# A hand-scheduled attention and expert block on one core: the layout products of z move to the bank of the weighted values, and the two tables of steps are laid out anew

## The chip, the cores and the metric

One NeuronCore of a Trainium2 chip runs the whole program. TensorE (PE) multiplies, VectorE (DVE), ScalarE (ACT) and GpSimd (POOL) do the rest, SyncE (SP) starts most transfers. The metric is the device time of one execution in microseconds, the median of several runs; less is better.

## The reference

Two stages follow each other on x of 2 x 1024 tokens with 256 features, and all of it is float32:

```python
# first stage: cross-attention to 154 context rows, 16 heads of 16
xq  = ada_ln(x, cond);  xkv = ada_ln(ctx, cond)
q = xq @ Wq + bq;  k, v = split(xkv @ Wkv + bkv)
x = x + (softmax(q k^T / 4) v) @ Wp + bp
# second stage: evidence from the same context, a router and three experts
nx = layer_norm(x) * gamma + beta
w  = softmax((nx @ Wq2) (ctx @ Wk2)^T / 16);  evidence = w (ctx @ Wv2)
c  = concat(nx, evidence, cond)
p  = softmax(c @ router_W + router_b)
y  = sum_e p_e * (silu(c @ e_w1[e] + e_b1) @ e_w2[e] + e_b2)
g  = sigmoid(silu(c @ gate_w1 + gate_b1) @ gate_w2 + gate_b2)
x  = x + g * (y @ out_w + out_b)
```

## The kernel before, in words

The 2048 tokens are cut into 4 chunks of 512 tokens, a chunk into 4 blocks of 128. The first stage handles the 16 heads of a chunk in 4 groups of 4, so there are 16 groups `g`. Everything is planned by hand. `PARTS` gives each kind of step a letter and lists its steps in order; a string of letters is a table of steps. Every engine walks the same table with `walk` and does its own share of each step, so that the table alone sets the order of the work on all engines. Between engines there are semaphores only, and each engine works strictly in order.

The letters that matter here, with what PE does and who answers:

- `P` projects the queries of a group (six 128x512 products in two steps), ACT and DVE make the query halves (L734, L1042). `R` (`rows`) computes row scores of one block into the two banks `pair` (L1377), and DVE takes their maximum (L1032); the next `R` waits for it. `S` (`shift`) adds the four maxima to the queries' bank (L1385), DVE makes the shifted queries. `K` (`keys`) computes scores by key into one of two banks, ACT exponentiates (L744); a `K` waits for the exponential of the `K` two before. `A` (`av`) sums the values weighted by the exponentials into the bank `B_U` (`bank4`; L1417, L1420), and ACT copies it to `u` (L753).
- `u` (`uz`) transposes one block's `u` (L1432), DVE divides and writes `z` (L1050, L1053). `z` (`ztr`) transposes that `z` (L1443), ACT copies it to `zt` (L759). `w` (`wproj`) multiplies `zt` by Wp, DVE adds it to x (L1059). These three are the layout products and the output product of a block, 16 blocks in all.
- `f` (`prep`, 29 of them) prepares weights of the second stage, `x` transposes a normalised chunk, `m` and `t` make the tables of the evidence product, `L`, `l`, `N` the second layer norm, `C`, `E`, `W`, `T`, `p` the evidence weights, `o` the router. `H` (`hidden`) is one of 14 blocks of a chunk's first expert layer (ten 128x512 products), `h` (`hsplit`) splits its result in two on DVE and POOL, `D` (`part`) is its second layer (twelve 128x256 products), `U`, `B`, `Z` sum and finish. `X`, `a`, `e` (`scale`, `gated`, `last`) finish the last chunk.

PSUM has eight banks. `B_TOK` (`bank5`) is shared by `f`, `x`, the first four `m`, and by `u`, `z` and `w` of the first 12 blocks. On PE the function `take_tok` guards it: whoever takes the bank first waits until the last user's result has been read. The last four blocks alternate between `B_TOK` and `B_U` (`tok_bank`). `B_U` belongs to `A` alone until then.

There are three tables: `L0_ORDER` (first stage and what was woven in), `BETWEEN_ORDER` (the passage: the last four blocks of the first stage, the evidence tables, the first evidence weights), `L1_ORDER` (the second stage). After `BETWEEN_ORDER` the first `H` needs, among other things, the low parts of the evidence tables that POOL moves between partitions with two DMAs (`m_ev<-m_ev`, L614). PE's products all go through the helper `passes`, so most of them have the line L1269.

Of the kernel before, what the change touches and what calls it, by code (L numbers as in the profile page):

```python
# [83 lines left out]
def build(nc, dram, out):  # L84
    ctx = ExitStack()
    with ctx:
# [244 lines left out]
        def y_tile(j):  # L331
# [4 lines left out]
            "s": [("split", c, h) for c in range(0, NC) for h in range(2)],  # L336
            "c": [("kc", gi) for gi in range(NG)],
            "V": [("val", n) for n in range(2)],
            "r": [("kr", gi) for gi in range(NG)],
            "P": [("proj", g, k) for g in range(GR) for k in range(KC)],  # L340
            "f": [("prep", n) for n in range(len(PREP))],
            "R": [("rows", g, q) for g in range(GR) for q in range(TJ)],
            "q": [("wq", 1)],
            "S": [("shift", g) for g in range(GR)],
            "K": [("keys", g, k) for g in range(GR) for k in range(GH + 1)],
            "b": [("stats", c, h) for c in range(1, NC) for h in range(2)],
            "g": [("rsqrt", c) for c in range(1, NC)],
            "A": [("av", g) for g in range(GR)],
            "n": [("norm", c, h) for c in range(1, NC) for h in range(2)],
            "y": [("second", n) for n in range(6)],  # L350
            "x": [("xt", c, h) for c in range(1, NC) for h in range(2)],
            "u": [("uz", n) for n in range(TJ * NC)],
            "z": [("zt", n) for n in range(TJ * NC)],
            "w": [("wp", n) for n in range(TJ * NC)],
            "m": [("m", n) for n in range(len(MP))],
            "t": [("m_taken", n) for n in range(len(MP))],
            "L": [("ln_stats", c) for c in range(NC)],
# [6 lines left out]
            "T": [("wtr", n) for n in range(TJ * NC)],  # L364
            "p": [("wsplit", c) for c in range(NC)],
            "o": [("router", c) for c in range(NC)],
            "H": [("hidden", c, m) for c in range(NC) for m in HORD],
            "i": [("w2_split", e) for e in range(E)],
            "h": [("hsplit", c, m) for c in range(NC) for m in range(HB)],
            "G": [("gate", n) for n in range(TJ * NC)],  # L370
            "D": [("part", c, m) for c in range(NC) for m in range(HB)],
            "B": [("bias", c, e) for c in range(NC - 1) for e in range(E)] + [("bias", NC - 1, e) for e in (0, 2, 1)],
# [6 lines left out]
        L0_ORDER = (  # L379
            "sscVcrPPfRqfRcVRcrPfPRfSffrrKRbKfRKKfRPKRbfPSfgRKA"  # L380
            "fKRPKKKRfRnA"
            "SfPyfKxnKRyKRxysKRKfRA"
            "sSPPfKPRKKfRyKyfKbRA"
            "yRfPSuKKRKuPKRzPfRwRbKSzA"
            "uKRKwPguKRKzKRPnwRA"
            "zSwnRKxKRKsxKRKsfA"
            "RPSPfKfRPKRKfKRbKfRPA"
            "SfKKRuKRKuKRzPRwPuSA"
            "zbRPzgRKwRKKwKRuKnPSzKnRxA"
            "wKRKxsKRsKfRPPSmtKA"  # L390
            "KRKfKRKmRA"
            "RPtPSfRKKuKRKzKRwPLPRuA"
            "SRzKKwKRKuPKRzlPwRuSRA"
            "KzRKKRKwRKA"
            "SmltNKKFtNmKCKCKEWEA"
            "CC"
        )
        BETWEEN_ORDER = (
            "TuWmztmuw"
            "mEWtmEtTzTWmtw"  # L400
            "Tputtmmztw"
            "umzotw"
        )
        L1_ORDER = (
            "H"
            "LlH"
            "H"
            "H"
            "NihGlhiDGihhH"
            "H"  # L410
            "NFBH"
            "GH"
            "hEDCGDCUhUUUEDH"
            "EWBCDH"
            "hCDWTH"
            "ThDWH"
            "hUUEUDhUH"
            "DWTDhpThLBH"
            "lUZH"
            "H"  # L420
            "DhUUH"
            "DH"
            "GNloUFhZH"
            "hNGDH"
            "H"
            "hZZDGhBDH"
            "ChUCUDUWEEUH"
            "hWH"
            "GH"
            "hCDTEBCWDhUH"  # L430
            "DhUUUWTDTEH"
            "poDTDhhLBUUH"
            "H"
            "DH"
            "lZDGhZH"
            "lH"
            "UGNUhH"
            "FNZH"
            "hDCZH"
            "CEhBhDH"  # L440
            "WDDGUhH"
            "UUUBEH"
            "EDEGhCCWDH"
            "hWUTUhUUDDH"
            "WhpTH"
            "TBTDH"
            "hoH"
            "DhH"
            "DUUDUH"
            "ZhZUGH"  # L450
            "hH"
            "ZhH"
            "GDZDhDBGUUH"
            "DH"
            "hUH"
            "UDH"
            "BH"
            "hDhBDhUXhDH"
            "H"
            "UUhhGUXH"  # L460
            "aXXhaaeaDeDeeDD"
        )
        part_of = {letter: iter(steps) for letter, steps in PARTS.items()}
        L0_STEPS = [next(part_of[letter]) for letter in L0_ORDER]
        BETWEEN_STEPS = [next(part_of[letter]) for letter in BETWEEN_ORDER]
# [57 lines left out]
        def _(pool):  # L523
# [85 lines left out]
            walk(L0_STEPS, {"xt": xb, "keys": keys, "av": av, "rsqrt": newton, "ln_stats": lambda c: newton(NC + c)})  # L609


            pool.wait_ge(m_h, m_hi(MTAIL))
# [646 lines left out]
        def _(pe):  # L1259
# [412 lines left out]
```

## Time and profile before

| | |
|---|---|
| time, 3 runs | 469.65, 471.16, 471.36 us; median 471.16 |
| time of the profiled execution | 471.39 us |
| its span (first to last instruction) | 469.6 us |
| PE busy | 445.7 us, 95% |
| DVE, ACT, POOL busy | 314.5, 215.5, 149.4 us |
| from the first key projection to the first `H` | 21.27 to 239.85 us |
| second stage on PE | 239.85 to 464.1 us |

The profiled execution took 1.8 us more than its span. A PE that is shown busy is one that has a product in flight: the busy time of a product reaches past the moment at which the next one may start.

### The profile page before, as it was taken

To read this page: it belongs to the slowest core of one execution; us is meant where nothing else is said; L and a number is where in the kernel's file an instruction comes from. 1 tells how busy PE (TensorE), PEld (TensorE's weight loads), DVE (VectorE), ACT (ScalarE), POOL (GpSimd) and SP (SyncE) were. 2 spreads that over 40 slices of the span, in tenths; PEclk is the share of its full clock that TensorE was granted. 3 is DMA by queue.
4 is the path that set the end of the run, shared out by engine and by line. 5 is a ranking of instruction groups with operands and counts; after the bars stand their busy time and mean duration, and the time that the engine had idled before them with its cause. 6 is when DMAs were issued, how large, how long until landed. Compare 5 with 4: busy or idle time off the path is not lost.

```text
span 469.6 us, 7042 instructions
## 1 busy us (share of the span) xinstructions
PE 445.7 (95%) x2396; PEld 345.7 (74%) x2396; DVE 314.5 (67%) x822; ACT 215.5 (46%) x377; POOL 149.4 (32%) x233
## 2 busy tenths in 40 slices
PE   7989889998999999999989999999999999999995
PEld 6866546665766657655468988889898889888885
DVE  5487676778568748858967687567776496733634
ACT  2466766455445545455432464254482355522220
POOL 4000263347343301200033224345225432334436
PEclk8599999999999999999999999999999999999998
DMA  8910411200220000000020000001000010001001
GB/s 285 398 29 1 156 46 46 68 24 22 68 67 3 0 1 0 1 1 1 0 75 1 1 0 1 1 1 46 0 1 1 1 45 1 1 1 45 1 0 46
DMA packets 7314, 17.50 MB, mean 37 GB/s; under 512 B 752, under 2 KB 2288, under 8 KB 7152
## 3 DMA queue, kind: packets, MB, share of 16 engines
q1 hardware_dynamic: 6336, 13.84, 8.4%
q0 software_dynamic: 656, 2.29, 1.7%
q10 hardware_dynamic: 288, 0.92, 0.5%
q8 instruction: 20, 0.33, 0.3%
q14 instruction: 14, 0.11, 0.1%
HBM read 14.50 MB, written 2.10 MB: 35 GB/s over the span
## 4 chain that ended last, share of the span: by engine, by line
PE 85%; DVE 5%; ACT 3%; DMA 2%; issue 2%; POOL 1%; POOLq 0%; SPq 0%; DVEq 0%; ACTq 0%
PE bank L1269 55%; PE pair L1269 14%; PE pair L1377 4%; PE bank L1420 3%; PE bank L1417 3%; DVE xq L1042 2%; DVE nm L1032 2%; DMA wss_sb<-in_wss 1%; PE bank L1432 1%; PE bank L1284 1%; PE bank L1385 1%; ACT xq L734 1%; DMA m_ev<-m_ev 1%; PE bank L1443 1%; ACT kc L680 1%
## 5 line engine op out<-in xcount | busy, mean ns | idle before, releaser
L620 POOL TENSOR_TENSOR hs<-hid,hs 128x512 fp32r<-128x512 f32 x48 | 63.4, 1320 | 114.7 <-DVE hs L1202 114.7
L1269 PE MATMUL bank<-nx,w1h 128*128 128x512 f32 x224 | 72.6, 405 | 0.2 <-DMA m_ev<-m_ev 0.2
L1269 PE MATMUL pair<-w2h,hs 128*128 128x256 f32 x384 | 72.1, 287 | 0.0
L1032 DVE TENSOR_REDUCE nm<-pair 128x4 fp32r<-128x616 f32 x64 | 51.1, 798 | 20.1 <-PE pair L1377 19.3
L1269 PEld LDWEIGHTS pair<-w2h,hs 128*128 128x128 f32 x384 | 60.9, 189 | 2.1 <-POOL hs L620 0.2
L815 ACT ACTIVATE hid<-bank,ab 128x512 f32<-128x512 f32 x48 | 33.0, 688 | 62.0 <-PE bank L1269 61.5
L1269 PE MATMUL pair<-w2l,hs 128*128 128x256 f32 x192 | 54.1, 282 | 0.0
L744 ACT ACTIVATE pt<-bank 128x512 f32<-128x512 f32 x72 | 41.0, 597 | 21.7 <-PE bank L1269 21.2
L1269 PEld LDWEIGHTS bank<-nx,w1h 128*128 128x128 f32 x224 | 39.9, 189 | 7.7 <-issue 0.8
L1269 PE MATMUL bank<-nx,w1l 128*128 128x512 f32 x112 | 44.2, 394 | 0.0
L1269 PE MATMUL bank<-wh,m_ev 128*128 128x512 f32 x112 | 44.1, 394 | 0.0
L1269 PE MATMUL bank<-xq,keys 128*128 128x512 f32 x96 | 39.6, 452 | 2.0 <-DVE xq L1042 1.6
L1377 PE MATMUL pair<-keys,xq 128*128 128x308 f32 x128 | 33.9, 346 | 5.4 <-DVE nm L1032 3.8
L1202 DVE CAST hs<-hid 128x512 fp32r<-128x512 f32 x48 | 22.7, 473 | 20.5 <-ACT hid L815 14.8
L1269 PEld LDWEIGHTS pair<-w2l,hs 128*128 128x128 f32 x192 | 36.1, 188 | 0.0
L1222 DVE SCALAR_TENSOR_TENSOR acc<-pair,pr,acc 128x256 f32<-128x256 f32 x44 | 19.6, 479 | 21.5 <-PE pair L1269 21.5
L1377 PEld LDWEIGHTS pair<-keys,xq 128*128 128x128 f32 x128 | 21.5, 189 | 16.5 <-issue 12.4
L568 POOL MEMSET xq<- 64x512 f32 x14 | 7.3, 520 | 81.0 <-PE bank L1269 80.9
L734 ACT ACTIVATE xq<-bank,small_sb 64x512 fp32r<-64x512 f32 x32 | 21.9, 683 | 20.1 <-PE bank L1269 19.6
L1042 DVE SCALAR_TENSOR_TENSOR xq<-bank,small_sb,xq 64x512 fp32r<-64x512 f32 x32 | 24.0, 750 | 9.1 <-PE bank L1385 8.3
L1269 PEld LDWEIGHTS bank<-wh,m_ev 128*128 128x128 f32 x112 | 21.0, 188 | 5.0
L1269 PEld LDWEIGHTS bank<-nx,w1l 128*128 128x128 f32 x112 | 21.0, 188 | 4.9
(209 smaller groups left out, 897.0 us busy)
## 6 DMA issues: line engine op xcount, KB each, us to landing
stage<-in_w1n POOLq DMA_DIRECT2D x7, 256.0 KB, 3.3
w1e_sb<-in_w1e SPq DMA_DIRECT2D x1, 1792.0 KB, 6.8
x_sb<-in_x SPq DMA_DIRECT2D x3, 512.0 KB, 10.3
stage<-in_w1a SPq DMA_DIRECT2D x3, 512.0 KB, 11.3
stage<-in_ew2T SPq DMA_DIRECT2D x3, 512.0 KB, 3.8
out_x<-x_sb SPq DMA_DIRECT2D x3, 512.0 KB, 2.6
wss_sb<-in_wss SPq DMA_DIRECT2D x2, 512.0 KB, 7.3
x_sb<-in_x ACTq DMA_DIRECT2D x1, 512.0 KB, 5.0
```

The lines of the kernel that those rows point to most:

```text
L620: g_.tensor_tensor(hs[:, q % 3, 1, :], hid[:, q % 2, :], hs[:, q % 3, 0, :], ALU.subtract).then_inc(hl_r, 1)
L734: A(xq[r, g % 2, s_, :], B_P[g % 2][r, :], ACT.Identity, bias=small[r, SM["bq"][0] + g % NG:SM["bq"][0] + g % NG + 1]).then_inc(qh_r, 1)
L744: A(weight(g, k), B_ST[n % 2][:, :], ACT.Exp, scale=DH ** -0.5).then_inc(ex_d, 1)
L815: A(dst, B_H[n % 2][:, :], ACT.Silu, bias=ab1[:, m, c // CPB:c // CPB + 1]).then_inc(h_r, 1)
L1032: V.tensor_reduce(nm[:, g % 2, q, :].rearrange("p (h w) -> p h w", w=32)[:, :, DH:DH + 1], pair[:, :, 0:2 * LK].rearrange("p s (a n) -> p ...
L1042: V.scalar_tensor_tensor(xq[low, g % 2, s_, :], B_P[g % 2][r, :], small[r, SM["bq"][0] + g % NG:SM["bq"][0] + g % NG + 1], xq[r, g % 2, s_ ...
L1202: V.tensor_copy(hs[:, q % 3, 0, :], hid[:, q % 2, :]).then_inc(hh_r, 1)
L1222: V.scalar_tensor_tensor(acc[:, j, :], y_tile(j), pr[:, c % 2, j, e:e + 1], acc[:, j, :], ALU.mult, ALU.add).then_inc(y_r, 1)
L1269: ins = mm(dst, a, b_, start=first and i == 0, stop=last and i == len(terms) - 1, skip_group_check=free)
L1377: ins = mm(B_S[s][:, 0:2 * LK], xq[:, g % 2, s, P * q:P * q + P], kr[c // CPB][:, gi, 2 * LK * s:2 * LK * (s + 1)], start=True, stop=True)
L1417: mm(B_U[32 * j:32 * j + 32, :], vmain[:, b, GH * gi + j, :], weight(g, j), start=True, stop=False, skip_group_check=True)
L1420: mm(B_U[:, :], vtail[:, b, gi, :], weight(g, GH), start=False, stop=True, skip_group_check=True).then_inc(av_d, 1)
```

## The change

The transposes of z (`ztr`) of the first 12 blocks write to `B_U` instead of `B_TOK`. On PE, `B_U` gets a guard of its own, `take_u`, used by `av` and by these transposes: each waits until ACT has read what the last user left there. The first two tables become one, `EARLY_ORDER`, and both tables have a new order; the order of the letters in `PARTS` has no effect. `gated` names one more wait on DVE, for the gate's tanh. The steps themselves are the same: each engine executes the same instructions on the same shapes.

```diff
         def tok_bank(n, step):
-            return B_TOK if n < LAST else (B_TOK, B_U)[(3 * (n - LAST) + step) % 2]
+            return (B_U if step == 1 else B_TOK) if n < LAST else (B_TOK, B_U)[(3 * (n - LAST) + step) % 2]
...
-        L0_ORDER = (
-            "sscVcrPPfRqfRcVRcrPfPRfSffrrKRbKfRKKfRPKRbfPSfgRKA"
...
-        BETWEEN_ORDER = (
...
+        EARLY_ORDER = (
+            "ssVcVrqPPfRbcfRcfRbcPfRrPSfRrgfKRKfKKRfrKRfPPSfKRKA"
...
+            "CtETCmuWmtzmtEuwtmTzmWouwttmztmwutTTptmzw"
         )
         L1_ORDER = (
...
             def gated(j):
 
                 dve.wait_ge(y_r, TJ * (E * NC - 2) + j + 1)
+                dve.wait_ge(th_r, TJ * (NC - 1) + j + 1)
...
+            ub = [None, None]
+
+            def take_u(freed, value):
+
+                if ub[0] is not None:
+                    pe.wait_ge(ub[0], ub[1])
+                ub[0], ub[1] = freed, value
...
                 if g == 0:
                     pe.wait_ge(v_r, B)
                     pe.wait_ge(ones_r, 1)
-                else:
-                    pe.wait_ge(u_r, g)
+                take_u(u_r, g + 1)
...
             def ztr(n):
                 if n < LAST:
-                    take_tok(zt_r, n + 1)
+                    take_u(zt_r, n + 1)
                 else:
                     pe.wait_ge(x1_r, n)
```

On every engine one walk replaces the walks of `L0_STEPS` and `BETWEEN_STEPS`.

**PE, first chunk.** The rows below are those of PE where the first blocks are turned while groups 4 and 5 run; `negI,nm` is a shift, `xq,keys0` a key score, `pair<-keys0,xq` a row score, `pt,vmain` and `pt,vtail` an `A`, `ident_sb,u` a `u`, `ident_sb,z` a `z`, `wp_sb,zt` a `w`. Before:

```order
L1269 MATMUL bank2<-xq,keys0 128x512 x2
L1385 MATMUL bank1<-negI,nm 128x128 x4
L1443 MATMUL bank5<-ident_sb,z 128x128 x2
L1417 MATMUL bank4<-pt,vmain 32x512 x4
L1420 MATMUL bank4<-pt,vtail 128x512
L1432 MATMUL bank5<-ident_sb,u 128x128 x4
L1269 MATMUL bank3<-xq,keys0 128x512
L1377 MATMUL pair<-keys0,xq 128x308 x2
L1269 MATMUL bank2<-xq,keys0 128x512
L1269 MATMUL bank5<-wp_sb,zt 128x256 x2
L1269 MATMUL bank1<-xh,wqh 128x512
```

The same place of the changed kernel:

```order
L1431 MATMUL bank5<-ident_sb,u 128x128 x4
L1385 MATMUL bank1<-negI,nm 128x128 x4
L1442 MATMUL bank4<-ident_sb,z 128x128 x2
L1377 MATMUL pair<-keys0,xq 128x308 x2
L1431 MATMUL bank5<-ident_sb,u 128x128 x4
L1416 MATMUL bank4<-pt,vmain 32x512 x4
L1419 MATMUL bank4<-pt,vtail 128x512
L1261 MATMUL bank3<-xq,keys0 128x512
L1377 MATMUL pair<-keys0,xq 128x308 x2
L1261 MATMUL bank5<-wp_sb,zt 128x256 x2
L1442 MATMUL bank4<-ident_sb,z 128x128 x2
```

The transposes of z stand in `bank4`, in turns with `A`, and a `u` may now follow a `u` in `bank5` with the `z` of the first between them.

**PE, the end of the passage.** The rows in front of the first `H` (`nx0,w1h`); `w1e_sb,vt` 64x256 is the last tail piece, whose result goes through ACT and POOL's two DMAs to the first `H`, and `ident_sb,pn` with `pn3` is a `T`. Before:

```order
L1269 MATMUL bank2<-w1e_sb,vt 64x256 x2
L1443 MATMUL bank4<-ident_sb,z 128x128 x2
L1269 MATMUL bank5<-wp_sb,zt 128x256 x2
L1432 MATMUL bank4<-ident_sb,u 128x128 x4
L1269 MATMUL bank3<-w1e_sb,vf 128x256 x2
L1443 MATMUL bank5<-ident_sb,z 128x128 x2
L1269 MATMUL bank4<-wp_sb,zt 128x256 x2
L1269 MATMUL bank2<-nx0,w1h 128x512 x2
```

The same place of the changed kernel:

```order
L1261 MATMUL bank2<-w1e_sb,vt 64x256 x2
L1261 MATMUL bank5<-wp_sb,zt 128x256 x2
L1431 MATMUL bank4<-ident_sb,u 128x128 x4
L1549 MATMUL pair<-ident_sb,pn 128x128
L1550 MATMUL pair<-ident_sb,pn3 96x128
L1549 MATMUL pair<-ident_sb,pn 128x128
L1550 MATMUL pair<-ident_sb,pn3 96x128
L1261 MATMUL bank3<-w1e_sb,vf 128x256 x2
L1442 MATMUL bank5<-ident_sb,z 128x128 x2
L1261 MATMUL bank4<-wp_sb,zt 128x256 x2
L1261 MATMUL bank2<-nx0,w1h 128x512 x2
```

Two `T` have moved in behind the tail piece, and the transpose of z that stood right behind it has moved ahead of it.

**DVE, the end of the program.** `acc<-th,acc` is a `gated`, `acc<-pair,lsc` a `last`, the cast the last `hsplit`; POOL adds to x in the same order. Before:

```order
L1235 TENSOR_SCALAR lsc<-th,pr 128x256 x2
L1202 CAST hs<-hid 128x512
L1240 SCALAR_TENSOR_TENSOR acc<-th,acc 128x256 x2
L1247 TENSOR_TENSOR acc<-pair,lsc 128x256
L1240 SCALAR_TENSOR_TENSOR acc<-th,acc 128x256
L1247 TENSOR_TENSOR acc<-pair,lsc 128x256 x3
```

The same place of the changed kernel:

```order
L1227 TENSOR_SCALAR lsc<-th,pr 128x256
L1233 SCALAR_TENSOR_TENSOR acc<-th,acc 128x256
L1194 CAST hs<-hid 128x512
L1233 SCALAR_TENSOR_TENSOR acc<-th,acc 128x256
L1240 TENSOR_TENSOR acc<-pair,lsc 128x256 x4
```

The last `gated` stands ahead of all four `last`, and the third one ahead of the last cast.

## Rows read from the trace of the kernel before

**Rows 1.** Page, busy time of each engine over the span, with instructions

```profile
PE 445.7 (95%) x2396; PEld 345.7 (74%) x2396; DVE 314.5 (67%) x822; ACT 215.5 (46%) x377; POOL 149.4 (32%) x233
```

**Rows 2.** Windows: start:end, width, then PE, PEld, DVE, ACT, POOL busy, clock

```profile
233.70:239.85 6.15, 4.38 (x22) 2.91 (x21) 5.23 (x17) 2.77 (x7) 1.13 (x2) 1.00 0.32 76
239.85:464.10 224.25, 224.21 (x1296) 196.81 (x1296) 141.33 (x404) 89.16 (x136) 83.52 (x100) 1.00 0.03 10
...
21.27:239.85 218.58, 203.05 (x1034) 133.47 (x1033) 161.57 (x361) 120.45 (x232) 56.90 (x115) 1.00 0.11 35
```

**Rows 3.** Waits of PE between 21 and 240 us: total, times, longest

```profile
PE pair L1377 <- DVE nm L1032: 3.8, 8, 0.8
PE bank L1269 <- DVE xq L1042: 1.6, 3, 0.9
...
PE bank L1420 <- ACT pt L744: 0.2, 1, 0.2
```

**Rows 4.** Timeline of group 4: start, duration, engine and line, waits in brackets

```profile
88.25 1.53 DVE L1042 SCALAR_TENSOR_TENSOR xq<-bank,small_sb,xq 64x512 fp32r<-64x512 f32 x2 [0.88 <-PE bank L1385]
89.05 0.73 PE L1269 MATMUL bank<-xq,keys 128*128 128x512 f32 x2 [0.38 <-DVE xq L1042]
89.59 1.09 ACT L744 ACTIVATE pt<-bank 128x512 f32<-128x512 f32 x2 [0.35 <-PE bank L1269]
...
92.08 0.45 PE L1377 MATMUL pair<-keys,xq 128*128 128x308 f32 x2
...
92.36 0.38 PE L1443 MATMUL bank<-ident_sb,z 128*128 128x128 f32 x2
...
92.56 0.80 DVE L1032 TENSOR_REDUCE nm<-pair 128x4 fp32r<-128x616 f32 x1 [0.50 <-PE pair L1377]
```

**Rows 5.** Groups by shape: count, busy time and mean ns, idle before

```profile
L744 ACT ACTIVATE pt<-bank 128x512 f32<-128x512 f32 x72 | 41.0, 597 | 21.7 <-PE bank L1269 21.2
...
L753 ACT ACTIVATE u<-bank 128x512 f32<-128x512 f32 x16 | 9.6, 598 | 26.4 <-PE bank L1420 26.4
...
L759 ACT ACTIVATE zt<-bank 128x256 f32<-128x256 f32 x16 | 6.1, 383 | 9.2 <-PE bank L1443 9.2
```

**Rows 6.** Timeline of the end of the passage

```profile
233.67 0.44 PE L1443 MATMUL bank<-ident_sb,z 128*128 128x128 f32 x2
...
234.43 0.36 ACT L769 ACTIVATE m_ev<-bank 32x256 fp32r<-32x256 f32 x1
...
234.81 0.38 ACT L770 ACTIVATE m_ev<-bank 32x256 fp32r<-32x256 f32 x1
...
235.55 0.60 PE L1432 MATMUL bank<-ident_sb,u 128*128 128x128 f32 x4
...
235.99 1.03 PE L1269 MATMUL bank<-w1e_sb,vf 128*128 128x256 f32 x4
...
239.85 0.70 PE L1269 MATMUL bank<-nx,w1h 128*128 128x512 f32 x2 [0.20 <-DMA m_ev<-m_ev]
```

**Rows 7.** Chain that ended last, pieces of it: start, us, what

```profile
236.40 3.31 DMA m_ev<-m_ev
...
286.19 2.32 PE bank L1269 x10
288.50 1.43 PE pair L1269 x12
```

**Rows 8.** Chain that ended last, behind the last product

```profile
463.89 0.83 POOL x_sb L637
464.73 0.68 POOL x_sb L631
465.41 0.68 POOL x_sb L637
```

**Rows 9.** The four `gated` on DVE: min/median/max ns, first and last start

```profile
L1240 DVE SCALAR_TENSOR_TENSOR acc<-th,acc x4: 415/416/1517, 457.8 to 463.7; 128x256 f32<-128x256 f32 x4
```

**Rows 10.** Timeline of POOL, the last `hsplit`

```profile
460.39 1.41 POOL L620 TENSOR_TENSOR hs<-hid,hs 128x512 fp32r<-128x512 f32 x1 [1.31 <-DVE hs L1202]
```

More of the change, by code:

```diff
@@ L364, in build @@
             "T": [("wtr", n) for n in range(TJ * NC)],
+            "o": [("router", c) for c in range(NC)],
             "p": [("wsplit", c) for c in range(NC)],
-            "o": [("router", c) for c in range(NC)],
             "H": [("hidden", c, m) for c in range(NC) for m in HORD],
@@ L428, in build @@
[L428 to L450, printed above, removed]
@@ L451, in build @@
-            "hH"
[L452 to L461, printed above, removed]
+            "LH"
+            "iH"
+            "H"
+            "hllH"
+            "hBFH"
+            "hNDNH"
+            "CiECGDhWWUH"
+            "H"
+            "EhDDUhGEUCCUBH"
+            "iEhH"
+            "GDTDhTWWH"
+            "UUhLDhUDUH"
+            "TH"
@@ new lines, in build @@
+            "pTlH"
+            "DBlH"
+            "hhGoNH"
+            "FhNH"
+            "DDUH"
+            "EUhEUDCUZCH"
+            "H"
+            "DH"
+            "DZWH"
+            "TWhH"
+            "hZZhBGEhEUDhUDCUCUTH"
+            "WBGhWH"
+            "DDH"
+            "hLhGphUUUDH"
+            "UlTTDH"
+            "GlDhBNUDH"
+            "oFUDDZNH"
+            "ZH"
+            "hCEUCH"
+            "hUGH"
+            "H"
+            "H"
+            "DhDZWEZhDCBH"
@@ L462, in build @@
+            "UhUCUDETUWH"
+            "hhH"
+            "GTH"
+            "EGDDhBH"
+            "WUWDhDUUpTH"
+            "TH"
+            "hUGoDH"
+            "hDH"
+            "H"
+            "DhDhBUUUH"
+            "ZGUhhZH"
+            "H"
+            "DZGDhhH"
+            "GZH"
+            "XDBUUUDGhH"
+            "UH"
+            "DH"
+            "BDBXH"
+            "DDH"
+            "hH"
+            "hhDhDXUDUaahUUXahDaeeee"
         )
         part_of = {letter: iter(steps) for letter, steps in PARTS.items()}
-        L0_STEPS = [next(part_of[letter]) for letter in L0_ORDER]
@@ L465, in build @@
-        BETWEEN_STEPS = [next(part_of[letter]) for letter in BETWEEN_ORDER]
+        EARLY_STEPS = [next(part_of[letter]) for letter in EARLY_ORDER]
         L1_STEPS = [next(part_of[letter]) for letter in L1_ORDER]
@@ L1251, in _ @@
             out_parts = {"uz": uz, "wp": wproj, "m_taken": mpiece}
[L1252 removed]
+            walk(EARLY_STEPS, {"kc": kc_, "kr": place, "wq": wq_split, "second": second, "val": val, "stats": chunk_stats, "rsqrt": chunk_rsqrt, "norm": norm, "split": xsplit, "rows": rows, "shift": shift, "prep": prep,
                               **out_parts, **front_parts})
[L1254 removed]
             walk(L1_STEPS, {"gate": gate, "w2_split": w2_split, "hsplit": hsplit, "bias": bias, "sum": expert_sum, "final": final, "scale": scale, "gated": gated, "last": last, **front_parts})
```

79 lines of the change are left out of this document (26 added, 53 removed).

## The prediction

> **What bounds the kernel now.** The page comes first: PE is busy 445.7 of 469.6 us, 95%, and DVE 67% [rows 1]. One number for the whole program hides two stages, so the windows come next. From the first `H` to PE's last product it is busy 224.21 of 224.25 us [rows 2]: the second stage is PE's own work, and an order can't shorten it unless it opens gaps. The early part, from the first key projection to the first `H`, lasts 218.58 us, of which PE is busy 203.05 [rows 2]. Its 15.5 us of visible gaps are what a new order can win.
>
> More is lost there than shows. The chain has ten 128x512 products in 2.32 us and twelve 128x256 products in 1.43 us [rows 7], so their slots are 0.23 and 0.12 us. The timeline shows a 128x512 product alone as 0.40 us and more: the last 0.17 us of it lie under the next one's slot when there is no gap. A gap of PE is therefore about 0.17 us longer than it is drawn.
>
> Then the waits: no single one rules. The largest kind is the row score behind DVE's maximum, 3.8 us in 8 waits; the shifted queries have 1.6 us in 3, the copy of `zt` 1.4 us in 3 [rows 3]. Fourteen kinds with some 28 waits make up PE's idle time. So this is a kernel of many small replies that come a little late, and I judge the new table by how much work PE has between a question and its answer.
>
> **The early table: cover.** I take slots as above (0.14 us for a row-score product, from 92.08 to 92.36 for two [rows 4]; others read in the same way) and a reply time for each kind of handover, from the end of the asking slot. Row scores ask until 92.36, and the maximum runs from 92.56 for 0.80 us [rows 4]; with the start of the next product and some queue on DVE I take 1.3 us. A key score asks at 89.28, ACT's exponential starts at 89.59 and takes 0.60 [rows 4, 5]: 1.15 us. A shift is answered by DVE's 0.77 us, and PE goes on 1.0 us later when it waits (88.05 to 89.05 [rows 4]): 1.3 us with some queue. Of the token bank I take 0.9 us behind a `z` (0.38 on ACT [rows 5]) or a `w`, 1.2 behind a `u`, 1.0 behind a preparation, 1.6 behind a transpose of x. Then I go through both orders and add PE's slots between question and answer:
>
> - row score to the next row score, 63 handovers: 23 are short of 1.3 us before and 15 after, the sum of what is missing 10.1 us before and 4.1 after;
> - key score to the second next, 78: 19 short before, 6 after, 6.4 and 1.9 us;
> - shift to the first key score, 16: 7 and 3, 3.8 and 2.4 us;
> - last row score to shift, 16: 5 and 10, 2.2 and 4.0 us, the one kind that gets worse;
> - projection to the first row score: 7 and 9, 6.1 and 5.1 us;
> - from one user of the token bank to the next: 76 takings before, of which 42 short by 16.8 us together; 64 after (the 12 transposes of z are gone), 24 short by 5.4 us;
> - `B_U`: 15 before, none short; 27 after, 3 short by 0.5 us.
>
> A step that waits for several things counts once, with the largest lack: 48.6 us before, 25.5 after, 48% less. The sum is no time, since a gap that one wait opens covers the next. The scale comes from the trace: without the last 6.15 us, PE's gaps in the early part are (218.58 - 6.15) - (203.05 - 4.38) = 13.8 us, and with 0.17 us each for about 27 waits 18.4 us. If gaps fell in proportion, 8.7 us would go. They won't quite: a gap that vanishes takes cover from its neighbours, and DVE, busy 161.6 of 218.6 us here [rows 2], has its replies pushed closer together. Averaged over stretches of 10 us of PE work, what DVE or ACT has to do beyond PE is even slightly more in the new table than in the old. I take a little over half: **4.8 us**. Bounds: 0 (gaps only move) and 8.7 us.
>
> **The end of the passage.** Before, the last tail piece of the evidence table is multiplied until 233.67, its copies on ACT wait for a transpose's copy and end at 235.19, POOL starts the DMAs, the chain has their 3.31 us from 236.40, and the first `H` starts at 239.85, with 0.20 us of waiting for them [rows 6, 7]: 4.66 us from ACT's end, 6.18 from the product's. PE's work in these 6.18 us is only about 3.5 us (two `w`, two `z`, a `u`, the last product), the rest are waits for `z` and `zt`. In the new order the transpose is ahead of the tail piece, so ACT can begin 0.2 us after it instead of 0.76: 0.2 + 0.36 + 0.38 + 4.66 = 5.6 us. The two `T` moved in give 3.7 us of work, so the transfer becomes what ends last here, and PE should wait for it visibly, up to about 1 us. Gain: 0.5 us in the path and 0.2 us of work that is now under it, **0.7 us** (from 0 to 1.0). The evidence weights, split on ACT and DVE only behind the second `T`, take some 3.2 us with the `zt` copy behind them, from 2 us after the tail product: they are in time by 0.4 us, and would be next in line.
>
> **The second stage.** The same instructions, and at least as much cover for most (the closest `hidden` to its `part` has 4.2 us of work between them in place of 3.6). Before, nothing shows but 0.04 us. 0, and up to 1 us lost.
>
> **The tail.** Behind the last product the chain is POOL's: a `last` of 0.83 us, the fourth `gated` of 0.68, another `last` [rows 8]. The new order has that `gated` ahead of all `last`, and its DVE part too: **0.7 us** off the path. Against it stands that the third `gated` is now ahead of the last cast on DVE. A `gated` takes 0.416 us, but one took 1.517 [rows 9], started at 460.2, while POOL subtracted from 460.39 for 1.41 us [rows 10]. If that hits the third, the cast, POOL's subtraction and the last `part` are late by 1.1 us, less about 0.5 us of room. The term is then 0.7 - 0.6 = 0.1 us. I take 0.7, since by the order POOL has nothing to do when it starts. The Trainium skill has a rule on this that speaks against the change: by "GPSIMD Engine Reference", section "Specifications", GpSimd's SBUF interface is shared with VectorE and contends with DVE instructions that have two SBUF inputs, which a `gated` is. The trace agrees with its 1.517 against 0.416 us; the rule alone would make the tail 0.1 us, the order of the two engines 0.7.
>
> **Sum.** 4.8 + 0.7 + 0 + 0.7 = 6.2 us off 471.4, the profiled execution's own time (span 469.6 and 1.8 around it), 465.2. The median of the runs shown is 0.2 lower, 471.16. I predict 465.4 us.
>
> **Rivals.**
>
> *The gaps only move.* The new order has no less to do for DVE and ACT, and the replies have queues behind them which my counts don't know; the kind that gets worse, row score to shift, is in each of the 16 groups. For it: DVE's load, 74% of the early part [rows 2]. Against it: nearly every kind has more cover at once. Then only 0 to 0.7 us of the early table, and the rest: 471.2 - 1.5 = 469.7 us. Measured as no change (a difference under 0.5%, 2.4 us, is about what can't be told).
>
> *`B_U` becomes the queue.* Now `A` waits for a copy of `zt` and `z` for the copy of `u` (0.598 us [rows 5]), on an ACT that has exponentials of 0.597 us in its queue. Six of the 27 handovers have under 1.4 us of cover (0.7 to 1.38, 1.0 in the mean). With two exponentials ahead of the copy the answer takes 0.17 + 3 x 0.6 = 2.0 us, 1 us late, 6 us in all, and each delays an `A` with its whole group. It decides from the point at which such queues are the rule and the early table gains less than 3.6 us: with no gain in it 471.2 + 6 - 1.4 = 475.8, with a small one 474 us. Against it: before, ACT waits 26.4 us for PE's `A` [rows 5], so it is mostly free at that moment.
>
> *All of the cover counts.* The gaps fall in proportion or beyond, as they would if the short row scores also delayed everything behind them: 8.7 to 10 us, with 1.4 us for the ends: 461 us. Against it: DVE would then be at 77% in the early part.
>
> *The change does nothing by its bank.* The bank alone lifts the wait of a `z` for the token bank only where a `z` was short (10 of its takings, 3.2 us of lack); if the gain is there, most of it comes from the order. This shifts no time here.
>
> **How the numbers follow.** My forecast, 462.5 to 468.5, has 0.56; gaps that move, 469 to 471.5, 0.20; the queue on `B_U`, 472 to 476, 0.10; all of the cover, 459.5 to 462.5, 0.14. The first and the last are faster by over 0.5% (under 468.8): 0.70. Same 0.20, slower 0.10. The range leaves out the slow rival and the far end of the fast one: 460.5 to 471.3.
>
> **What would show it.** Right: the first `H` starts at about 234.4 us (239.85 - 5.5), PE's idle time in the early part falls from 15.5 to about 11 us; its waits for DVE's maximum are fewer; a wait of PE for `m_ev` of 0.3 to 1 us stands in front of the first `H`; 224.2 us follow with PE full; from PE's end to the end 4.8 us in place of 5.5, with no L1233 between the POOL pieces of the chain. Wrong: waits of `A` or `z` for ACT's `u` and `zt` of more than 2 us together (the queue), or the same idle time with other names (moved gaps), or gaps in the second stage.

## The result, and the profile after

The changed kernel takes 457.18 us (median of 4 runs, 456.38 to 458.20) against 471.16: a ratio of 0.9725, 95% interval [0.9674, 0.9775]. The forecast was 465.4, in a range of 460.5 to 471.3. The direction was right, the gain of 14 us was over twice the forecast 6.2, and the time lies below the range.

The windows of the profiled execution (458.2 us, span 456.2), columns as in [rows 2]; the first three rows go from PE's first product of the early table and from the first row score to the first `H`, and from there to PE's last product:

```profile
21.27:227.54 206.27, 198.67 (x1033) 136.12 (x1033) 163.18 (x362) 120.25 (x231) 56.31 (x115) 0.99 0.12 37
29.48:227.54 198.06, 190.96 (x1004) 130.08 (x1003) 156.88 (x346) 115.37 (x221) 56.31 (x115) 0.99 0.11 34
227.54:451.50 223.96, 223.95 (x1296) 196.88 (x1296) 145.53 (x403) 88.26 (x135) 85.09 (x101) 1.00 0.03 10
...
57.00:61.10 4.10, 2.43 (x12) 1.68 (x12) 3.33 (x6) 2.83 (x6) 3.31 (x6) 1.00 0.01 4
61.20:64.60 3.40, 3.40 (x13) 2.65 (x11) 1.83 (x3) 2.27 (x4) 0.50 (x1) 0.50 0.00 0
```

The early part lost 12.3 us (218.58 to 206.27), all behind the prologue. Two things stand out. PE's gaps fell from 15.5 to 7.6 us, which is only 7.9 of the 12.3: its busy time fell as well, from 203.05 to 198.67 us, for the same products. And from 61.2 to 64.6 us the granted clock is 0.50, the lower of its two levels, so 1.7 us are lost in a stretch that the kernel before doesn't have.

The waits of PE in the whole program:

```profile
PE pair L1377 <- DVE nm L1024: 2.5, 4, 1.5
...
PE bank L1261 <- DVE kc L959: 0.9, 2, 0.8
PE bank L1385 <- DVE nm L1024: 0.7, 2, 0.5
PE bank L1261 <- DMA m_ev<-m_ev: 0.7, 1, 0.7
PE bank L1261 <- ACT zt L752: 0.6, 1, 0.6
```

The maximum still leads, in 4 waits in place of 8 [rows 3]. No wait for ACT's `u` or for `B_U` is on the list. The chain that ended last, at the end of the passage and behind the last product:

```profile
222.49 0.38 ACT m_ev L763
...
223.48 0.60 POOL m_ev L607
...
224.09 3.32 DMA m_ev<-m_ev
...
227.54 1.63 PE bank L1261 x6
```

```profile
450.82 0.44 DVE acc L1240
...
451.32 1.40 POOL x_sb L630 x2
452.73 0.68 POOLq L86
453.41 0.68 POOL x_sb L630
```

ACT's second copy starts at 222.49 and the DMA ends 4.9 us later; the tail has no `gated` between its `last` pieces and takes 4.7 us in place of 5.5.

### The profile page after: what moved, and what is told of

It is laid out like the page before. It is cut to its first block, busy times and chain, and to the rows that moved or that the text cites. A ratio compares the mean times of both kernels' runs of the same rounds, so it can differ in the third digit from the quotient of the medians.

```text
span 456.2 us, 7055 instructions
## 1 busy us (share of the span) xinstructions
PE 441.0 (97%) x2396; PEld 348.5 (76%) x2396; DVE 320.0 (70%) x822; ACT 214.4 (47%) x377; POOL 149.6 (33%) x233
## 4 chain that ended last, share of the span: by engine, by line
PE 89%; DVE 4%; DMA 2%; ACT 2%; issue 1%; POOL 1%; POOLq 0%; SPq 0%; DVEq 0%
PE bank L1261 55%; PE pair L1261 15%; PE pair L1377 4%; PE bank L1419 3%; PE bank L1416 3%; DMA wss_sb<-in_wss 2%; PE bank L1431 2%; PE bank L1385 1%; ACT kc L673 1%; DVE nm L1024 1%; PE bank L1276 1%; PE bank L1316 1%; DVE kc L959 1%; DMA m_ev<-m_ev 1%; PE bank L1442 1%
## 5 line engine op out<-in xcount | busy, mean ns | idle before, releaser
L1194 DVE CAST hs<-hid 128x512 fp32r<-128x512 f32 x48 | 21.6, 458 | 34.3 <-ACT hid L808 22.3
L1261 PE MATMUL bank<-xq,keys 128*128 128x512 f32 x96 | 39.4, 466 | 0.2
L1377 PE MATMUL pair<-keys,xq 128*128 128x308 f32 x128 | 35.2, 357 | 2.9 <-DVE nm L1024 2.5
L727 ACT ACTIVATE xq<-bank,small_sb 64x512 fp32r<-64x512 f32 x32 | 21.8, 682 | 18.9 <-PE bank L1261 18.4
```

The costliest lines, as they stand in the source:

```text
L727: A(xq[r, g % 2, s_, :], B_P[g % 2][r, :], ACT.Identity, bias=small[r, SM["bq"][0] + g % NG:SM["bq"][0] + g % NG + 1]).then_inc(qh_r, 1)
L1194: V.tensor_copy(hs[:, q % 3, 0, :], hid[:, q % 2, :]).then_inc(hh_r, 1)
L1261: ins = mm(dst, a, b_, start=first and i == 0, stop=last and i == len(terms) - 1, skip_group_check=free)
L1377: ins = mm(B_S[s][:, 0:2 * LK], xq[:, g % 2, s, P * q:P * q + P], kr[c // CPB][:, gi, 2 * LK * s:2 * LK * (s + 1)], start=True, stop=True)
```

## A measure for the loss, used below

The experiments are compared on one stretch, from the first row score to the first `H`: 211.06 us before, 198.06 after. The prologue is left out, since its length differs between runs of one and the same kernel: the clock is at its lower level there for a time that varies. The windows of before, and of an experiment with the new order:

```profile
10.00:15.00 5.00, 5.00 (x19) 3.96 (x19) 4.24 (x22) 0.11 (x1) 0.00 (x0) 0.50 1.04 404
15.00:20.00 5.00, 5.00 (x22) 4.60 (x22) 0.99 (x5) 2.23 (x6) 0.00 (x0) 0.50 1.05 396
```

```profile
10.00:15.00 5.00, 5.00 (x24) 4.03 (x24) 4.14 (x22) 0.98 (x3) 0.00 (x0) 0.66 1.05 405
15.00:20.00 5.00, 5.00 (x25) 4.38 (x25) 2.25 (x8) 3.29 (x8) 0.00 (x0) 0.69 1.05 396
```

The first is the kernel before, the second order_only. In the profiled executions this lower level lasts from 3.4 to 13.7 us, which at half the speed is up to 5.1 us of time; 30 runs of the kernel before on one chip went from 466.42 (mean clock 0.993) to 471.59 us (0.982). Ahead of the first record of the clock, 4.3 to 7.3 us into the full kernels, 128x512 products start 0.43 us apart instead of 0.23, so PE is at the lower level there too; this time isn't in these figures.

What PE would need without any late reply was measured by itself (`pe_alone`, below): 182.24 us for this stretch in the old order, 180.82 in the new. The difference to the full kernel is its **loss**. "Lack" is the sum of missing cover by the forecast's count, "low" the time at the lower clock inside the stretch, of which half is lost; it is 1.7 us wherever 3.4 stands.

| kernel | ratio to before, 95% | stretch, us | low | loss | lack |
|---|---|---|---|---|---|
| before | 1 | 211.06 | 0 | 28.8 | 48.6 |
| changed | 0.9725 [0.9674, 0.9775] | 198.06 | 3.4 | 17.2 | 25.5 |
| changed_again | 0.9694 [0.9624, 0.9764] | 198.33 | 3.4 | 17.5 | 25.5 |
| bank_only | 1.0074 [1.0042, 1.0106] | 215.54 | 3.4 | 33.3 | 51.0 |
| order_only | 0.9917 [0.9881, 0.9953] | 207.10 | 3.4 | 26.3 | 36.2 |
| late_only | 0.9997 [0.9960, 1.0034] | 211.03 | 0 | 28.8 | 48.6 |
| new_to_a8 | 0.9900 [0.9863, 0.9938] | 204.45 | 0 | about 23 | 39.4 |
| norm_later | 0.9700 [0.9648, 0.9752] | 198.22 | 3.4 | 17.4 | 25.5 |
| short_max_before | 0.9931 [0.9897, 0.9964] | 206.72 | 0 | 24.5 | 38.1 |
| short_max_after | 0.9617 [0.9565, 0.9669] | 194.85 | 3.4 | 14.0 | 18.4 |
| climbed | 0.9676 [0.9623, 0.9729] | 196.19 | 0 | about 15 | 25.0 |
| least_lack | 0.9727 [0.9672, 0.9783] | 196.75 | 0 | 16.0 | 15.6 |
| one_bank_least | 0.9954 [0.9917, 0.9990] | 210.66 | 0 | about 29 | 31.0 |

("About": the order was not run alone, and 181 or 182 us are taken for it.)

Since PE's products come in one order, the loss can be taken apart: for each product, the distance to the one before it in the full kernel less the same distance in PE alone, summed by the step that the product belongs to. Worked out from the starts of some 790 products (those that start together counted once) (in us; `R` row scores, `K` key scores, `S` shifts, `prep` preparations; `rest` has projections, table pieces, scores and the first `H`):

```
                    R    K    S    A  prep   u    z    w    x  rest   sum
before             8.5  4.0  0.5  0.2  6.6  1.9  1.6  2.7  0.4  2.4  28.8
bank_only          8.2  3.8  0.5  2.3  6.6  2.8  3.8  2.3  0.7  2.4  33.3
short_max_before   2.1  4.7  0.1  0.6  7.7  2.2  1.6  3.0  0.4  2.0  24.5
order_only         5.9  1.1  1.4  0.1  3.6  2.2  6.2  2.4  1.8  1.6  26.3
changed            6.6  1.1  1.6  0.1  3.3  0.7  0.1  1.7  0.5  1.5  17.2
short_max_after    3.8  1.7  0.4  0.1  3.6  0.7  0.0  1.5  0.5  1.8  14.0
least_lack         4.4  0.8  0.9  0.1  5.1  0.7  1.3  1.1  0.5  1.1  16.0
```

## The experiments

**The bank without the order, the order without the bank.** In both, one half of the change; the bank's half is

```diff
-            return B_TOK if n < LAST else (B_TOK, B_U)[(3 * (n - LAST) + step) % 2]
+            return (B_U if step == 1 else B_TOK) if n < LAST else (B_TOK, B_U)[(3 * (n - LAST) + step) % 2]
```

> The kernel before with one thing of the change: the twelve layout products of z below the last chunk write to `B_U` and take it in turn with `A`; both tables keep the order of before, and the fourth `gated` waits for the hyperbolic tangent as in the changed kernel. Theory *cover*: what counts is how much PE work lies between a question and its answer. In the old order z on `B_U` relieves the token bank but its neighbours on `B_U` are now too close (4.3 us of lack appear there), so the sum of what is missing goes from 48.6 to 51.0 us; at the 0.5 us of time per us of lack that the pair of kernels shows (11.7 us for 48.6 - 25.5 = 23.1 us), 1.2 us slower: 472.4 us, between 471 and 474. Rival *bank*: the token bank's queue was the cause, and the new order only follows it: then most of the 14 us is here already, under 463 us.

> The changed kernel with one thing taken back: the layout products of z use the token bank again, in both tables' new order. Theory *cover*: in this order 64 takings become 76, and z stands close to `u` and `w`, so the lack goes from 25.5 to 36.2 us, and at 0.5 us per us 5.4 us of the gain are lost: 457.2 + 5.4 = 462.6 us, between 460 and 465. PE's waits for the copies of `zt` and of z then show in the trace. Rival *bank*: without the second bank the new order gains next to nothing: over 468 us. Rival *order alone*: the bank's place doesn't matter, 457 to 459 us.

The bank alone made the kernel 0.7% slower: the queue on `B_U` that the prediction named as a rival is real in the old order. Its waits of PE (the experiments' line numbers are 64 below those of the changed kernel, as their tables stand on fewer lines):

```profile
PE bank L1378 <- ACT u L682: 1.8, 3, 0.7
...
PE bank L1352 <- ACT zt L688: 1.4, 1, 1.4
```

The first is a `z` behind the copy of `u`, the second an `A` (here L1352) behind the copy of `zt`, and a slow stretch of the clock follows it at 97.0 us (that the wait brought it is not shown):

```profile
95.00:97.00 2.00, 0.57 (x7) 0.31 (x11) 1.90 (x6) 1.72 (x4) 1.81 (x3) 1.00 0.04 8
97.00:100.40 3.40, 3.40 (x10) 0.73 (x3) 0.28 (x1) 0.00 (x0) 1.30 (x2) 0.50 0.29 75
```

```profile
96.82 1.83 PE L1352 MATMUL bank<-pt,vmain 128*32 128x512 f32 x8 [1.43 <-ACT zt L688]
98.59 2.01 PE L1355 MATMUL bank<-pt,vtail 128*128 128x512 f32 x2
```

The order alone gives 0.8%, less than the 462.6 us expected (1.8%). Without the bank, `z` (L1378) waits for DVE's division (L981), which also frees the token bank of the `u` before it, and for the residual addition, `u` (L1367) and x (L1252) for `zt`:

```profile
PE bank L1378 <- DVE z L981: 2.1, 4, 0.8
PE bank L1378 <- DVE x_sb L987: 1.6, 3, 0.8
...
PE bank L1367 <- ACT zt L688: 1.1, 2, 0.8
PE bank L1252 <- ACT zt L688: 1.1, 1, 1.1
```

So the two halves are no sum: on this stretch +4.5 and -4.0 us alone, -13.0 together (without the slow stretches of the clock +2.8, -5.7 and -14.7). The new table puts `u`, `z` and `w` close to one another, which needs the second bank; the old one puts `z` right ahead of `A`, where the second bank hurts. The rival that the bank alone is the cause and the rival that it doesn't matter both fall.

**The second table alone, and the new order up to the eighth `A`.**

> The kernel before with the second table of the changed kernel only, and its wait in `gated`; early tables and bank of before. Theory: the second stage is PE's own work in either order, and only the tail gets shorter, by the `gated` that POOL no longer does between its `last` pieces: 471.2 - 0.8 = 470.4 us, between 469.7 and 471; in the trace PE's end lies 4.7 us before the end of the span, in place of 5.5. Rival: part of the gain of 13 us lies in the second table, below 468 us.

> A table that follows the new order up to the eighth `A` and then has the steps that are left in the old order, z on `B_U`, second table of before. Theory *cover*: the sum of lack is 39.4 us, 9.2 less than before, so at 0.5 us per us 4.7 us faster: 466.5 us, between 464.5 and 468.5. Rival *one place*: the gain stems from one stretch (the first half, say); then this kernel has all of it (under 460) or none (over 470).

The second table leaves the time where it was within [0.9960, 1.0034], too wide for 0.8 us; its profile has 223.95 us in the second stage and, from PE's last start to the end, 5.1 us in place of 5.8. With the new order up to the eighth `A`, 1.0% is gained, as expected, and 6.6 of the 13.0 us of the stretch: half of the gain lies up to there and half behind it, not all in one place.

**The long wait of the new table.** At 58 to 60 us the largest wait is left. The timeline of the changed kernel:

```profile
54.61 0.74 DVE L876 TENSOR_SCALAR lnt<-x_sb,mv,rs 128x256 f32<-128x256 f32 x2
...
57.80 0.39 DVE L959 SCALAR_TENSOR_TENSOR kc<-bank,small_sb,klo 64x154 fp32r<-64x154 f32 x1
...
58.22 1.41 DVE L876 TENSOR_SCALAR lnt<-x_sb,mv,rs 128x256 f32<-128x256 f32 x2
...
59.65 0.80 DVE L1024 TENSOR_REDUCE nm<-pair 128x4 fp32r<-128x616 f32 x1
...
60.60 0.52 PE L1377 MATMUL pair<-keys,xq 128*128 128x308 f32 x2 [1.49 <-DVE nm L1024]
```

```diff
-            "nKRfnRKKPfRPxSRKKfyKRssxA"
+            "nKRfRnKKPfRPxSRKKfyKRssxA"
```

> The changed kernel itself once more, beside the kernel before on the same chip, since the profiles show PE's clock at its lower level for a stretch of the prologue whose length differs from run to run (3.4 us up to 13.7 us), and once more at 61.2 to 64.6 us in the changed kernel, behind a wait of 1.5 us. Theory: that second stretch belongs to the kernel's order and comes again; 457 us, 2.9% below the kernel before, with 189.4 us from the first shift to the first `H` (201.4 before). Rival: it is chance; without it the same stretch of the program takes 187.7 us.

> The changed kernel with one letter of the early table moved: the normalising of the second half of chunk 1 behind the row score (2,2), no longer ahead of it. In the changed kernel it took 1.41 us on DVE there, and PE waited 1.49 us for the maximum behind it, after which the granted clock was 0.5 for 3.4 us. Theory *wait and clock*: the 1.5 us of waiting go and with them the slow stretch, which costs as much again (3.4 us at half the speed, 1.7 us): together 3 us less than the changed kernel, 454 us. Rival *the wait only*: 1.4 us less. Rival *it moves*: the normalising delays the next reply by as much, no change.

The changed kernel came out the same on another chip, slow stretch included (55.6 us, since the prologue was shorter). Moving the letter did what the third rival said: the wait for the maximum went, and one of the same size came at the transposes of x, whose bank waits for the key block that DVE now makes later. Between 40 and 70 us:

```profile
PE bank L1252 <- DVE kc L895: 1.2, 1, 1.2
PE bank L1197 <- DVE kc L895: 1.0, 2, 0.8
PE pair L1313 <- DVE nm L960: 0.6, 2, 0.4
```

**A shorter maximum, with both orders untouched.**

```diff
-                                pair[:, :, 0:2 * LK].rearrange("p s (a n) -> p s a n", a=2), AXX, ALU.max).then_inc(mx_d, 1)
+                                pair[:, :, 0:2 * LK].rearrange("p s (a n) -> p s a n", a=2)[:, :, :, 0:38], AXX, ALU.max).then_inc(mx_d, 1)
```

> The kernel before with the row maximum taken over 38 of the 154 keys of a head (so it leaves out part of the maximum, which sets only the shift of the exponentials). The maximum takes 0.80 us, this one should take some 0.25, so every answer to a row score comes 0.55 us sooner, with the order untouched. Theory *cover*: what is missing falls from 48.6 to 38.1 us, at 0.57 us of time per us of lack (13.1 us for 23.1, the changed kernel without its slow stretch) 6.0 us faster: 465 us against 471. Rival *DVE is no cause*: PE's gaps come from elsewhere, under 2 us. Rival *DVE's queue*: 35 us less of DVE's work help every other reply too, over 9 us.

> The same shortened row maximum (38 of 154 keys, part of the maximum left out) in the changed kernel. Theory *cover*: the new order already covers most of the row scores, so less is left to win: the lack falls from 25.5 to 18.4 us, 4.0 us faster, and the slow stretch behind the wait of 1.5 us may go as well (1.7 us): 451 to 453 us. Rival: as much as in the kernel before or more, and then the new order's gain has nothing to do with how late the maxima are.

The maximum by groups, before and then shortened with the old order:

```profile
L1032 DVE TENSOR_REDUCE nm<-pair 128x4 fp32r<-128x616 f32 x64 | 51.1, 798 | 20.1 <-PE pair L1377 19.3
...
L1032 DVE TENSOR_REDUCE nm<-pair 128x4 fp32r<-128x152 f32 x64 | 20.1, 314 | 22.3 <-PE pair L1377 21.5
```

0.31 us in place of 0.80, and the stretch is 4.3 us shorter with the old order, 3.2 to 3.5 with the new. Expected were 6.0 and 4.0. With the old order neither rival holds, under 2 us or over 9; with the new one the gain is less than with the old, so its rival falls too. The row scores alone lose 6.4 us less (8.5 to 2.1), and a third of it, net, comes back, 1.1 at the preparations, 0.7 at the key scores, 0.3 to 0.4 each at `u`, `w` and `A`: this is the cover that a vanished gap takes from its neighbours. The table also says that the row scores lose nearly as much in the new order as in the old (6.6 and 8.5), though by the count their lack had fallen by 7 us.

**PE alone.** All blocks but PE's are taken out; DVE clears two shared tiles and raises every semaphore by 100, then PE's program runs as it stands.

```diff
+            for s in SEMS:
+                nc.vector.memset(flag[:], 0.0).then_inc(s, 100)
+                dve.wait_ge(s, 100)
```

> PE's program of the kernel before, with all its waits, and nothing else: no other engine computes, all operands are zeros in two shared tiles, every semaphore is raised far enough before PE starts, so each wait is answered long before it is asked (the kernel computes nothing of the reference; it leaves out all work of the other engines). It gives the time of PE's own slots, which the timeline of the full kernel can't show. Theory *late replies*: from the first shift to the first `H` 160 us, against 201.4 in the full kernel: 41 us are late replies, not the 18.4 of the forecast. Rival *the forecast's scale*: about 183 us, and the loss is what the drawn gaps say.

> The same for the changed kernel: PE's program with all its waits, every one answered before it is asked, all work of the other engines left out. Theory *late replies*: within 2.5 us of the order of before (158 to 160 us from the first shift to the first `H`), so the new order gains by replies and not by PE's own work. Rival *PE's own slots*: what stands next to what on PE sets the cost (a waiting step behind a transpose, say), and the new order is quicker by 5 us or more here already.

> As the one before, but without the waits of PE's program (only the first, for the zeros). The difference is what waits cost that are answered long before: about 320 more instructions for waits in PE's queue. Theory: some 0.08 us for each step with two waits or more, as a row score behind a key score starts 0.31 us after it in place of 0.23, so 10 to 20 us shorter over the whole program, most of it in the early part. Rival: waits that are answered cost nothing, no difference.

The windows of the stretch, in this order of kernels, the first with its second stage below it:

```profile
59.09:241.32 182.23, 182.23 (x1008) 130.25 (x1007) 0.00 (x0) 0.00 (x0) 1.00 0.00 1
241.32:464.80 223.48, 223.48 (x1298) 197.68 (x1296) 0.00 (x0) 0.00 (x0) 1.00 0.00 1
```

```profile
63.14:243.96 180.82, 180.82 (x1004) 129.49 (x1003) 0.00 (x0) 0.00 (x0) 1.00 0.00 1
```

```profile
60.39:241.19 180.80, 180.80 (x1004) 129.48 (x1003) 0.00 (x0) 0.00 (x0) 1.00 0.00 1
```

From the first shift on it is 173.7 and 173.2 us. My 160 was wrong, and so was the forecast's scale. The two orders differ by 1.4 us in PE's own slots, and a wait that is answered costs nothing (180.82 against 180.80), against my theory of 10 to 20 us. The row to look at beside it is that of the full kernel before:

```profile
28.79:239.85 211.06, 196.82 (x1007) 128.44 (x1007) 155.91 (x346) 114.13 (x218) 56.90 (x115) 1.00 0.10 32
```

PE counts as busy for 196.82 us there, where PE alone is busy 182.23 with the same products. So of the 28.8 us lost, 14.2 are drawn as gaps and 14.6 hide under the drawn ends of products.

PE alone also differs in that the other engines are still and its operands are zeros, so a rival is that they slow PE's products themselves. The starts speak against it. In the second stage, where DVE, ACT and POOL work too, the full kernel takes 224.25 us [rows 2] and PE alone 223.48, and of 1296 products 3 start more than 0.02 us late, 0.2 us together; in the changed kernel none does. In the early part 860 of 1006 products of the kernel before start within 0.02 us of their distance in PE alone, and all 49 that are late by more than 0.17 us are products whose weight load waits for a semaphore. Each of the programs with PE alone was executed once, so 1.4 us between two orders rests on one execution of each; the two in the new order and the one of least_lack, below, agree within 0.1 us.

**A table with the tangle at 56 to 60 us undone.** The letters of that place, changed kernel and experiment:

```
"...KRfPPSfKRKA"  "nKRfnRKKPfRPxSRKKfyKRssxA"
"...KRfPPSRnfKKA" "RfnKRKPfRKPxSRKKfsyKRsxA"
```

> The changed kernel with some twenty letters of the early table moved by one to five places, most of them between 38 and 62 us: the score products of group 1 go on while DVE and ACT prepare the keys of the second batch, and their placing stands apart from the row maxima. By the count of cover nothing changes: 25.0 us are missing in place of 25.5, 0.3 us faster. Theory *count*: 0 to 1 us faster than the changed kernel. Rival *queues*: the count knows no queues on DVE and ACT; where several replies stand behind one another on DVE (key blocks, normalising, maximum at 56 to 60 us), untangling them gives 3 to 5 us, and with no gap of over a microsecond the slow stretch of the clock goes as well.

The stretch is 196.19 us with no slow part: 2.1 less than changed_again, of which 1.7 are the clock. In the ratio (0.9676 against 0.9694) it can't be told from the changed kernel. What was left at this place wasn't 3 to 5 us.

**Tables made by the count itself.** By then loss over lack, with the 1.7 us of the slow stretches taken off, was 0.58 to 0.68 in every kernel. The next tables were made by lowering the lack alone; their expectations are the most informative misses of this study.

> The changed kernel with an early table in which 72 of 379 letters stand elsewhere, each by a few places, chosen for nothing but a smaller sum of missing cover, by the reply times of the forecast: 15.6 us are missing in place of 25.5 (48.6 before). Theory *count*: PE loses 0.61 us per us of lack, 9.5 us from the first row score to the first `H` in place of 15.6; that stretch takes 190.3 us in place of 196.4, and the kernel is 6 us faster than the changed one, 1.3%: a ratio to the kernel before of 0.956. Rival *floor*: what is left in the changed kernel is queues and the fixed price of handovers, which no count sees; under 2 us faster. Rival *read in afterwards*: a table made for the count opens waits that the count doesn't know, and is slower.

> The layout products of z stay in the token bank, as before, and the early table is the old one with some 60 of 379 letters elsewhere, chosen for nothing but a smaller sum of missing cover with one bank: 31.0 us in place of 48.6; second table of the change. Theory *count*: 0.61 x 31.0 = 18.9 us lost in place of 28.8, and 0.8 us of the tail: 10.7 us faster than the kernel before, a ratio of 0.977, so that an order alone gives three quarters of the change's gain once it is made for one bank. Rival *bank*: without the second bank the token bank's queue stays the limit, and it comes out like the new order without the bank, 5 us faster, 0.99.

> PE's program of the kernel least_lack alone, with all its waits answered before they are asked, all work of the other engines left out. In the full kernel the stretch from the first row score to the first `H` takes 196.75 us. Theory *late replies*: PE alone needs 179 to 181.5 us for it, as in the changed kernel's order (180.8), so 15 to 18 us are still late replies, though the count had 9.5. Rival *PE's own slots*: the many small moves made PE's own program dearer, 185 us or more, and its replies cost the 9.5 to 11 us of the count.

Neither gained what was expected: least_lack comes out at the changed kernel's ratio instead of 1.6% below it, one_bank_least 0.5% under the kernel before instead of 2.3%, of which 0.8 us (0.2%) would be the tail. With 15.6 us of lack the stretch is 196.75 us, 16.0 above PE alone in that order:

```profile
63.26:243.99 180.73, 180.73 (x1004) 129.49 (x1003) 0.00 (x0) 0.00 (x0) 1.00 0.00 1
```

With 31.0 us of lack and one bank, 210.66 us, where before had 211.06. The loss over lack is 1.0 and 0.9. By kinds, least_lack wins 2.2 us at the row scores over the changed kernel and loses 1.8 at the preparations and 1.2 at z. The timeline shows one reason that the count couldn't see, the preparation of a key block of the second batch:

```profile
51.88 0.70 PE L1197 MATMUL bank<-xkv,wk_sb 128*128 128x160 f32 x4
...
52.62 0.48 ACT L607 ACTIVATE klo<-bank,small_sb 128x154 fp32r<-128x154 f32 x1 [0.23 <-PE bank L1197]
...
53.12 0.98 ACT L609 ACTIVATE kc<-bank,small_sb 64x154 fp32r<-64x154 f32 x2
...
54.20 0.77 DVE L895 SCALAR_TENSOR_TENSOR kc<-bank,small_sb,klo 64x154 fp32r<-64x154 f32 x2 [0.72 <-ACT kc L609]
...
55.12 0.78 PE L1197 MATMUL bank<-xkv,wk_sb 128*128 128x160 f32 x4 [0.97 <-DVE kc L895]
```

The reply takes 2.6 us, its operations on ACT and DVE one behind the other; the count had 1.0 us for every preparation. Counted again with this (2.7 for the four of them), the lack is 51.1 before, 29.1 changed, 19.8 here and 33.7 with one bank, and the loss is still 0.8 to 0.9 of it in the two made tables, against 0.56 before and 0.53 changed. So this is at most a part of it.

## Why the prediction was right in direction and wrong in size

**The whole.** The span fell by 13.4 us: 11.7 in the early table, 0.6 at the end of the passage, 0.3 in the second stage, 0.8 in the tail.

**Second stage, tail, end of the passage: right.** 223.95 us (forecast 224.2); tail 0.8 us shorter (0.7), with the `gated` ahead of the last subtraction and the cast not delayed: none of the four was slowed on DVE, they took 0.414 to 0.421 us; from the tail product at 221.99 to the first `H` 5.55 us (5.6), with the DMA as what ended last and a wait of 0.7 us for it (0.3 to 1). The first `H` came at 227.54, not 234.4, only because all before it was earlier.

**The early table: the term that failed.** "4.8 us" was 11.7 (212.40 us from the first product of the table to the tail product before, 200.72 after), beyond even its upper bound of 8.7. Two steps of it were wrong.

The *scale*: "with 0.17 us each for about 27 waits 18.4 us". PE alone gives 28.8 us in a shorter stretch. The correction for the drawn ends was right in kind but applied to the waits that the view lists. Of some 790 starts, 49 were late by more than 0.17 us (23.6 us together) and 90 more by 0.02 to 0.17 us (6.1 us), while the view lists 29 waits. Most of them leave no gap in the trace. In the changed kernel it is 28 (13.1 us) and 72 (5.2 us).

The *share*: "I take a little over half" of a proportional fall. The loss fell from 28.8 to 17.2 us, by 40%, and by 46% without the slow stretch, where the count said 48%. With the scale of 28.8 a fall in proportion, the rival "All of the cover counts", gives 13.7 us; measured are 13.3 without the slow stretch and 11.6 with it. To these 11.6 us come 1.4 us of PE's own slots, which the prediction didn't consider: another order of the same products is not equally long on PE.

**The count was roughly right as a ranking, not as a price.** By the prediction's own list the users of the two banks (`u`, `z`, `w`, x, preparations) had 10.9 us less lack and gave 6.9 us of loss; the key scores, with those behind a shift, 5.9 and 2.9; the row scores, with those behind a projection, 7.0 and only 1.9; the shift got worse by 1.8 and by 1.1. And the two tables made to lower the count gained next to nothing by it. It told tables roughly apart that were laid out by other means; it didn't hold as a price to be pushed down. It knows neither queues on DVE and ACT nor how long each reply takes; of these only the reply of the key blocks was found in a trace.

**The bank: half wrong.** "The change does nothing by its bank": so it is in the old order, where it costs 4.5 us of the stretch, 1.7 of them by the clock. In the new one it is worth 9.0 (207.10 to 198.06): 6.1 us at z, 1.5 at `u`, 1.3 at x, 0.7 at `w`. I had priced the bank in the old order only.

**The rival of `B_U`: wrong for this kernel,** right for bank_only, down to the wait of an `A` for `zt`. **"The gaps only move"** didn't happen in the whole, but norm_later and least_lack are cases of it, and short_max_before shows its rate, a third.

Four slips of the recorded text. PE's waits between 21 and 240 us are 16 kinds and 29 waits, not "fourteen kinds with some 28". The 1.4 us for the copy of `zt` are in that view, but not among the rows shown as [rows 3]. And the cover from row score to shift is not short "in each of the 16 groups", but in 10 of 16, by the prediction's own list. And its sum gives 471.16 - 6.2 = 465.0 us, not the 465.4 that it states.

**What stays open.** What brings the slow stretch near 55 to 62 us. It is there in all five profiled kernels with exactly the new table or one letter off it, and in none of those with the old one, with new_to_a8's, climbed's or the two made ones; so it goes with the table. But it isn't a matter of the table alone, nor of a late reply: PE alone shows it too, in pe_alone_after and pe_alone_least, with PE at work without a gap since 42.1 us, and not in pe_no_waits_after, which has the same products as the first. This is pe_alone_after:

```profile
54.50:58.10 3.60, 3.60 (x15) 3.15 (x14) 0.00 (x0) 0.00 (x0) 0.53 0.00 0
```

In these two the first products start 0.43 us apart until 47.8 and 48.0 us, in the two without it only until some 45 us; what ties the two stretches together no run shows. Nor is it settled what the made tables lose beyond the key blocks.

## What to carry to other kernels

Measure the bound before pricing the gain: the busiest engine's program alone, with every wait answered, gives its loss product by product, and here it was 28.8 us where the gaps of the trace showed 14.2. A count of cover is good for comparing tables and for finding places, but it is not a time, and the two tables tuned to it here ran into what it had left out. Where a change has an order and a resource, price the resource inside the new order; here one half alone brought less than a third of the gain, and the other made the kernel slower.

## What the hardware showed that I had not expected

A wait that is already answered costs PE nothing that can be measured: 180.82 us with all waits, 180.80 without. By the records the clock's lower level in the prologue lasted from 3.4 to 13.7 us in different executions, which moves the whole time by up to 5.1 us, more than most of the effects here; comparing a stretch behind it is sharper than comparing times. Two normalisings on DVE took 1.41 us beside POOL's additions at 58.22, and 0.74 us at 54.61 without them. The Trainium skill's page "GPSIMD Engine Reference", section "Specifications", speaks of contention with DVE instructions that have two SBUF inputs or run in a 2-port perf mode. This one has a single large input, so the trace would agree with the page only by the second case, and no run here shows in which mode it ran.
